# Adding the edge terms of a gathered message on VectorE instead of TensorE

## The reference

```python
def _L1_gnn_ref(H, Xe, id_Xe, M_W, M_b, U_W, U_b):
    features = H[id_Xe[0]]
    M_in = jnp.concatenate([features, Xe], axis=1)
    Y = jax.nn.relu(M_in @ M_W.T + M_b)
    Z = jax.ops.segment_sum(Y, id_Xe[1], num_segments=H.shape[0])
    U_in = jnp.concatenate([H, Z], axis=1)
    H_next = jax.nn.relu(U_in @ U_W.T + U_b)
    return H_next
```

## Time and profile before

| | |
|---|---|
| time, median of three runs | 26277.79 us (26254.98 to 26295.2) |
| the profiled execution: time | 26277.79 us |
| its span | 26276.0 us |
| PE busy | 9716.5 us (37%) |
| DVE busy | 9902.9 us (38%) |
| ACT busy | 1687.5 us (6%) |
| POOL busy | 15440.7 us (59%) |
| second gather layer, first gather to last block add | 4960 us |

### The profile page before, as it was taken

How to read it: one execution, slowest core, us unless ns; L and a number is a source line. 1 busy time by engine, 2 the same in 40 slices (tenths; PEclk the granted TensorE clock), 3 DMA queues, 4 the chain that set the end, 5 groups by cost and what they waited for, 6 DMA issues and landing times. The chain is left out here.

```text
span 26276.0 us, 210259 instructions
## 1 busy us (share of the span) xinstructions
PE 9716.5 (37%) x49375; PEld 7209.6 (27%) x49376; DVE 9902.9 (38%) x24717; ACT 1687.5 (6%) x4834; POOL 15440.7 (59%) x16460
## 2 busy tenths in 40 slices
PE   2555555423333333344343453333333111111146
PEld 1323232223333332222222223333333111111145
DVE  6666666533333333222222232222223222222257
ACT  4000000000000000000000010000000111111101
POOL 2666666666666664666666526666665666666610
PEclk7555555555555555666666665555555555555578
DMA  3222222222222222122121222222222222222255
GB/s 96 80 79 79 79 78 71 61 55 54 54 54 54 53 56 39 50 52 53 50 52 48 49 97 53 54 54 56 54 56 46 72 72 72 71 71 71 71 167 186
DMA packets 1005339, 1785.55 MB, mean 68 GB/s; under 512 B 352516, under 2 KB 461345, under 8 KB 1004756
## 3 DMA queue, kind: packets, MB, share of 16 engines
q1 hardware_dynamic: 484516, 1127.73, 13.6%
q0 software_dynamic: 513696, 654.80, 11.1%
q10 hardware_dynamic: 7056, 2.21, 0.0%
HBM read 1279.39 MB, written 510.79 MB: 68 GB/s over the span
## 5 line engine op out<-in xcount | busy, mean ns | idle before, releaser
L935 POOL DMA_INDIRECT arena<-table,arena x6464 | 6097.8, 943 | 3198.4 <-issue 1935.7
L1033 PE MATMUL psum<-arena 128*128 128x64 f32 x19392 | 4036.8, 369 | 8949.8 <-issue 7855.4
L1033 PEld LDWEIGHTS psum<-arena 128*128 128x128 f32 x19392 | 3960.5, 293 | 9289.3 <-issue 8978.6
L986 DVE TENSOR_TENSOR arena<-arena,psum 128x64 f32 x9696 | 2152.4, 222 | 9615.8 <-remote 4340.2
L700 POOL DMA_INDIRECT rec<-arena x3125 | 2991.6, 957 | 2284.4 <-issue 1847.9
L1150 POOL DMA_INDIRECT rec<-arena x3232 | 3178.9, 984 | 1770.2 <-issue 953.8
L935 POOL DMA_INDIRECT arena<-ptable,arena x3232 | 3048.9, 943 | 1871.2 <-issue 968.9
L477 PE MATMUL psum<-arena 128*128 128x196 bf16 (+1 forms) x4375 | 1378.6, 429 | 2174.4 <-DVE arena L608 1307.3
L1228 PE MATMUL psum<-arena 128*128 x3232 | 589.3, 362 | 3845.1 <-DVE arena L1177 2516.1
L1177 DVE CAST arena<-psum 128x1536 bf16<-128x1536 f32 x404 | 710.2, 1758 | 3407.8 <-remote 3352.6
L1228 PEld LDWEIGHTS psum<-arena 128*128 128x128 bf16 x3232 | 352.6, 109 | 4038.9 <-issue 3951.1
(11 more groups left out here) (198 smaller groups left out, 10158.6 us busy)
## 6 DMA issues: line engine op xcount, KB each, us to landing
arena<-rec SPq DMA_DIRECT2D x303, 1408.0 KB
arena<-rec SPq DMA_DIRECT2D x440, 488.0 KB
arena<-in_edge SPq DMA_DIRECT2D x625, 232.0 KB
arena<-rec SPq DMA_DIRECT2D x404, 352.0 KB
arena<-table,arena POOLq DMA_INDIRECT x6464
rec<-arena POOLq DMA_INDIRECT x6357
table<-arena SPq DMA_DIRECT2D x196, 512.0 KB
arena<-ptable,arena POOLq DMA_INDIRECT x3232
```

Of the source, the lines that this page charges most:

```text
L935: nc.gpsimd.indirect_dma_start(rows[q][:, j * D:(j + 1) * D], None, tab, bass.IndirectOffsetOnAxis(ap=idx[:, j, field:field + 1], axis=0)) ...
L986: v.tensor_tensor(block_sum, block_sum, ps[q % SB][:, j * D:(j + 1) * D], ALU.add).then_inc(s_add[j], 1)
L1033: last = nc.tensor.matmul(ps[q % SB][:, j * D:(j + 1) * D], hot[q % SB][:, j * P:(j + 1) * P], rows[q][:, j * D:(j + 1) * D], start=True, ...
```

## The change

The sum of gathered row and record term is made by the DVE, in place in `rows[q]`, as one 128x512 add (`add_terms`). It stands in the DVE's order of a group behind the one-hots of the group two on and ahead of the block adds of the group before. ACT takes the relu in place, from SBUF to SBUF. PE keeps only the products, in the same order in all layers. SP's wait for the one-hots of a block's last group is replaced by the wait for its sum in the second layer, which the DVE now gives. The banks `ps_q` and the parameter `ident` go.

```diff
-    ps_q = [psum[:, 512 * (SB + 1 + k):512 * (SB + 2 + k)] for k in range(2)]
...
-                    wait_earlier(sp, s_hot[q], i)
-                    if relu_q:
-                        wait_earlier(sp, s_sum[q], i)
+                    wait_earlier(sp, s_sum[q] if relu_q else s_hot[q], i)
...
+            def add_terms(i, q):
+                r = recs[q].rearrange("p (j w) -> p j w", w=RW)
+                mine = rows[q].rearrange("p (j f) -> p j f", f=D)
+                dve.wait_ge(s_g[q], i * (16 * G) + 16 * G)
+                v.tensor_tensor(mine, mine, r[:, :, R_Q:RW], ALU.add).then_inc(s_sum[q], 1)
+
             def step(i, groups=RG):
                 for q in range(groups):
                     if groups == RG or q + AHEAD < groups:
                         one_hots(i + (q + AHEAD) // RG, (q + AHEAD) % RG)
+                    if relu_q:
+                        add_terms(i, q)
                     if q:
                         add_group(i, q - 1)
...
                         act.wait_ge(s_sum[q], i + 1)
-                        nc.scalar.activation(rows[q], ps_q[q % 2], ACT.Relu).then_inc(s_msg, 1)
+                        nc.scalar.activation(rows[q], rows[q], ACT.Relu).then_inc(s_msg, 1)
...
-            def add_terms(i, q):
-                n = i * RG + q
-                pe.wait_ge(s_g[q], i * (16 * G) + 16 * G)
-                wait_earlier(pe, s_msg, n - 1)
-                nc.tensor.matmul(ps_q[q % 2], ident, rows[q], start=True, stop=False)
-                nc.tensor.matmul(ps_q[q % 2].rearrange("p (j f) -> p j f", f=D), ident,
-                                 recs[q].rearrange("p (j w) -> p j w", w=RW)[:, :, R_Q:RW], start=False, stop=True).then_inc(s_sum[q], 1)
...
             def step(i, groups=RG):
                 for q in range(groups):
+                    n = i * RG + q
+                    pe.wait_ge(s_hot[q], i + 1)
                     if relu_q:
-                        add_terms(i, q)
-                        if q:
-                            products(i, q - 1)
-                        elif not isinstance(i, int) or i:
-                            products(i - 1, RG - 1)
+                        pe.wait_ge(s_msg, n + 1)
                     else:
-                        products(i, q)
+                        pe.wait_ge(s_g[q], i * (16 * G) + 16 * G)
+
+                    wait_earlier(pe, s_add[G - 1], n - (SB - 1))
+                    for j in range(G):
+                        last = nc.tensor.matmul(ps[q % SB][:, j * D:(j + 1) * D], hot[q % SB][:, j * P:(j + 1) * P],
+                                                rows[q][:, j * D:(j + 1) * D], start=True, stop=True)
+                    last.then_inc(s_mm, 1)
```

More of the change, by code:

```diff
@@ L156, in build @@
         hparts, acc2 = shared.bitcast(BF16), shared[:, 0:NB * MW]
-        gather_layer(nc, sem, "g0", Buffers(arena, b.at), psum, iotaf, ident, blkd, acc, rec, table, R_GIDX, True, False)
+        gather_layer(nc, sem, "g0", Buffers(arena, b.at), psum, iotaf, blkd, acc, rec, table, R_GIDX, True, False)
         sem.end_stage()
@@ L160, in build @@
         sem.end_stage()
-        gather_layer(nc, sem, "g1", Buffers(arena, b.at), psum, iotaf, ident, blkd, acc, rec, ptable, R_SRC, False, True)
+        gather_layer(nc, sem, "g1", Buffers(arena, b.at), psum, iotaf, blkd, acc, rec, ptable, R_SRC, False, True)
         sem.end_stage()
@@ L166, in build @@
         sem.end_stage()
-        gather_layer(nc, sem, "g2", Buffers(arena, b.at), psum, iotaf, ident, blkd, acc, rec, table, R_GIDX, False, False)
+        gather_layer(nc, sem, "g2", Buffers(arena, b.at), psum, iotaf, blkd, acc, rec, table, R_GIDX, False, False)
         sem.end_stage()
@@ L883, in _, with gather_layer @@
                 step(last_pair, False)
-def gather_layer(nc, sem, name, b, psum, iotaf, ident, blkd, acc, rec, table, field, weighted, relu_q):
+def gather_layer(nc, sem, name, b, psum, iotaf, blkd, acc, rec, table, field, weighted, relu_q):
     loads = [b.take(LG * G * RW) for _ in range(RG // LG)]
@@ L1014, in _ @@
         def _(pe):
-            def add_terms(i, q):
-                n = i * RG + q
-                pe.wait_ge(s_g[q], i * (16 * G) + 16 * G)
-                wait_earlier(pe, s_msg, n - 1)
-                nc.tensor.matmul(ps_q[q % 2], ident, rows[q], start=True, stop=False)
-                nc.tensor.matmul(ps_q[q % 2].rearrange("p (j f) -> p j f", f=D), ident,
-                                 recs[q].rearrange("p (j w) -> p j w", w=RW)[:, :, R_Q:RW], start=False, stop=True).then_inc(s_sum[q], 1)
[L1023 to L1035, removed]
             def step(i, groups=RG):
                 for q in range(groups):
+                    n = i * RG + q
+                    pe.wait_ge(s_hot[q], i + 1)
                     if relu_q:
-                        add_terms(i, q)
-                        if q:
-                            products(i, q - 1)
-                        elif not isinstance(i, int) or i:
-                            products(i - 1, RG - 1)
-                    else:
-                        products(i, q)
+                        pe.wait_ge(s_msg, n + 1)
+                    else:
+                        pe.wait_ge(s_g[q], i * (16 * G) + 16 * G)
[4 more added lines that the diff above has]
+                    last.then_inc(s_mm, 1)
             peeled(pe, TURNS, step)
             step(TURNS, REST)
-            if relu_q:
-                products(TURNS, REST - 1)
 def update_stage(nc, sem, a, b, psum, ident, x, acc, h):
```

## The result

The kernel after took 26610.3 us (median of 4 runs, 26588.8 to 26618.9) against 26286.5 us before on the same chip (4 runs): ratio 1.0124, 95% interval 1.0106 to 1.0141, or 324 us more. The forecast was 26580 us, in a range of 26180 to 26870. The profiled execution had a span of 26630.0 us, 354 us more than the one before (26276.0).

A forecast was written before the change was run, and what follows sets the result against it. POOL's waits were taken to set the second gather layer's time; the later load and tail gave 252 to 290 us, taken as 300 with what both counts omit: 26278 + 300 = 26580 us, range 26180 to 26870.

The forecast's parts named there:

- What sets the layer's time: Second gather layer: what POOL waits for sets its time, 902 us of waits against 611 in the third layer.
- The wait that is moved: SP's load release in the second layer: 4.4 and 7.0 us later in two places, mean 5.7 us.
- The two counts: Later load in the second layer: 43 waits x 5.7 = 245 us, or 5.6 x 50.5 patterns = 283 us.
- The pattern of eight groups: POOL's stops per two loads: 9.85 us, then 13.6, together 23.5 us in eight groups against 17.9 before.
- The split of the waits: POOL in the second layer: waits for loads grow from 471.6 to some 750 us, for products stay at 430.
- The DVE's step in a burst: DVE in the second layer after a restart: 5.16 us a group becomes 5.9 with the new add.
- three new adds stand in the DVE's way: First place examined: 3 x 0.73 us of adds since the restart help let the load go 4.4 us later.
- the second count: Count by the pattern of eight groups: 23.5 us against 17.9, 5.6 x 50.5 = 283 us more.
- The add's price: New DVE add of 128x512 fp32 in the second layer: 688 ns, 0.73 us with the wait ahead of it.
- a gain of the change as written: Faster rival: second layer falls to the third's time, POOL's waits 902 to 611 us, 25994 us; chance 0.17.
- The tail: After POOL's last gather the DVE has some ten groups in hand, each 0.73 us longer: 7 us.
- The port: Rival: adds with two SBUF inputs block POOL's gathers, 279 us, 26557 us, or 26860 with the forecast on top; chance 0.08.

The follow-up runs named there:

- its removal in two different ways: Kernel after with the DVE's add made two groups ahead, ratio 0.9882; kernel after with second-layer loads of two groups instead of four, ratio 0.9898.
- the first: Kernel before, PE keeping the adds, SP's second-layer load also waiting for a small DVE memset where the change puts its add: 26755.1 us, ratio 1.0119.
- the fourth experiment: Kernel after with the add's second input taken from PSUM instead of SBUF, the record's term left out: 26669.0 us, ratio 1.0092.
- the terms ahead: Kernel after, but the DVE adds the terms of group q+2 right behind that group's one-hots: 26105.1 us, ratio 0.9882.
- the run made for it: Terms added two groups ahead, plus PE's eight records per group put back unused: 22713.2 us, ratio 1.0042; run again, 22696.2 us, 1.0046.
- 20 places: 20 places for groups instead of 12 in all gather layers, with the terms two groups ahead: 22702.2 us, ratio 1.0036.
- the repeat on the faster chip: Kernel after itself, unchanged, measured again where the kernel before took 22593.7 us: 22681.9 us, ratio 1.0039.
- the first four experiments: Later release alone, terms two groups ahead, loads of two groups, add's input from PSUM; run on one chip where before took 26428.5 us.
- the run with the marker in the third layer: Kernel before with loads released later, by a small DVE memset behind the one-hots two groups on, in the third gather layer alone: 22620.9 us, ratio 1.0000.

## Why the prediction was right

The time lies 30 us from the forecast, and the wait that the forecast rests on is the one that costs it. The sizes of its parts came out less well, and some of the errors cancel.

**What sets the layer's time.** Right: POOL's waits rose by 335 us and the layer by 382.

**The wait that is moved.** Right, and shown by itself: the later release alone gives 1.0119, its removal in two different ways gives 0.9882 and 0.9898. The two counts had 245 and 283 us for it; POOL's waits rose by 335. As forecast, the load is issued right behind the add of the block's last group.

**The pattern of eight groups.** Forecast 9.85 + 13.6 = 23.5 us of waits in eight groups; measured 1237 / 50.5 = 24.5. The mean hides two kinds: the pairs are 23.5 us, as drawn, though from other parts than drawn (see the DVE's step below), and more than half of the places are single stops of 26.4, which the pattern did not have. Where the add's second input comes from PSUM the pattern came in full (9.9 + 13.6).

**The split of the waits.** Off: 750 us for loads and 430 for products were forecast, 1053 and 184 measured. In the 27 single stops POOL stands at the load for the time that it would have stood at the product: the one wait hides behind the other. Only the sum was right.

**The DVE's step in a burst.** Wrong: 5.16 us should have become 5.9. Its one-hots start at 11592.50, 11597.63 and 11603.13, 5.1 and 5.5 us apart (5.25 over the five steps from 11592.50 to 11618.73). Before, the DVE stood idle some 1.2 us ahead of its block adds, put down to "issue" (it reads their eight places from memory); the idle time ahead of them is 0.62 us now. The add of 0.68 us lies in that gap. So in the step "three new adds stand in the DVE's way" the 0.73 us were mis-sized, they are near 0.1 a group. With 5.25 us in place of 5.9 the second count would have given 1.3 us less at each of 50.5 places, 66 us. That the sum came out all the same is luck in part. In 18 of the 22 pairs, and in all 48 of the run with the input from PSUM, the DVE stands before the load is let go, 2.5 us on average in that run, until a product of PE is made; the count had no such wait. And the 27 single stops are some 3 us longer than a pair.

**The add's price.** 0.688 us from the line through two rows; 684 ns measured. Hidden, as said. **ACT:** 630 ns, hidden.

**PE and the port, two terms put at nothing.** The sum had nothing for the work that PE loses and nothing for the port. On the slower chip PE's part was worth some 86 us with the late load (the first against the fourth experiment), and the port cost about as much, as far as ratios from two chips can be compared: 1.0124 against 1.0092. That they cancel is luck. With the terms ahead the second layer falls to the third's length, 1.2% under before. How much of this is the earlier load, how much PE's eight records and how much the post that PE no longer gives stays open: the run made for it fell on chips without stops. What did not come is a gain of the change as written; the late load hid it.

**The tail.** Seven us were added for the groups in hand after POOL's last gather. Measured, 53.0 us before and 53.8 after: under 1.

**The port.** The mechanism was given 0.08 and called not borne out, on one overlapping pair of rows. It is real, and the sign named for it came (gathers over 943 ns, here 956): the Trainium skill ("SBUF — State Buffer", section "Who interferes with whom") has it that such an instruction contends with a GpSimd instruction that reads SBUF, and the runs agree: 944 ns with the input from PSUM, 971 from SBUF. The size is not the rule's whole length: 88 us on the faster chip where the forecast's upper figure was 279, as only some gathers start while an add runs. Those lose nearly what is left of it, 0.41 us where they start 0.1 to 0.2 us into it. Nor does the later one always wait for what is left of the other: in the repeat on the faster chip an add that starts while a gather runs takes 700 ns on average, 723 at most, where 692 is the least. In the kernel after on the chip of the prediction the gathers themselves were 32 us longer for it (3090.1 busy against 3057.7 in the third layer), so it was no main term there. The error of the step was in the pair it looked at: that transfer started 0.21 us into an add of 0.29, so only 0.08 us of the add was left, and no more than that could be lost; gathers of the kernel after that start with so little left take 946 ns. The same stage of the trace before had the answer, at the DVE instruction behind that one, also with two SBUF inputs (L1173):

```profile
...
23804.35 0.30 DVE L1173 TENSOR_TENSOR arena<-arena 128x136 bf16<-128x136 f32 x1
23804.41 1.09 POOL L1150 DMA_INDIRECT rec<-arena  x1 [0.30 <-issue]
...
```

The 29 transfers of that stage that start 0.06 to 0.15 us into such an instruction take 1.01 to 1.09 us; the other transfers shown there and in the earlier trace rows take 0.98.

## What to carry to other kernels

When an instruction that frees a buffer moves to another engine, count where it stands in that engine's order, not only how long it takes: here a 0.7 us add cost 324 us because two groups of other work stood ahead of it, and the same add two groups earlier, with the loads then let go earlier than ever, gained 323. A ring of buffers is only as deep as its latest release. And read a loss on the machine that has it: where POOL never waited, the same edit cost a quarter as much and for another reason, and the terms-ahead version that wins 1.2% on one chip loses 0.4 to 0.5% on the others (measured there with 20 places and with PE's extra records, not alone).

## What the runs showed of the hardware

**The same program took 26255 to 26441 us in the runs of the result and of the first four experiments, and 22591 to 22634 on the two chips of the others.** In the slower runs PE goes through long stretches in which each of its records starts some 1.4 us behind the last. In the kernel before, on the first chip, PE's matmuls of the adds with their weight loads:

```profile
...
11560.19 1.01 PE L1019 MATMUL psum<-arena 128*128 128x512 f32 x1 [2.52 <-issue]
...
11561.59 0.29 PEld L1019 LDWEIGHTS psum<-arena 128*128 128x128 f32 x1 [2.51 <-issue]
...
11563.00 1.01 PE L1019 MATMUL psum<-arena 128*128 128x512 f32 x1 [1.79 <-issue]
...
11564.40 0.29 PEld L1020 LDWEIGHTS psum<-arena 128*128 128x128 f32 x1 [2.51 <-issue]
...
11566.49 1.01 PE L1020 MATMUL psum<-arena 128*128 128x512 f32 x1 [2.49 <-issue]
...
```

and in the run with the marker in the third layer, on a faster chip, at the same work (the add's second half, the products and the relu of the group):

```profile
...
10000.77 1.91 PE L1027 MATMUL psum<-arena 128*128 128x512 f32 x2
...
10002.47 2.08 PE L1040 MATMUL psum<-arena 128*128 128x64 f32 x16
...
10002.72 0.60 ACT L1016 ACTIVATE arena<-psum 128x512 f32<-128x512 f32 x1 [9.49 <-PE psum L1027]
...
```

From the first to the last of these records 6.3 us pass on the slower chip; on the faster one the two matmuls of a line took 1.91 us together, and the relu follows PE 0.04 us after their end. On the slower chip the relu often starts long after the sum that it waits for: in the kernel before, 154 of the 404 relus began more than 5 us after the end of the group's last L1020 matmul, up to 83 us; in the run on the faster chip all 404 began 0.04 us after it. And the DVE and POOL restart together, 9.85 us, 9.80 us and, in the kernel after, 9.42 us after POOL has stopped. What these stretches are (what PE's records wait for) was not settled; that they do not come from the program alone is shown by the faster chips.

**A gather and an add of two SBUF inputs on the DVE.** Gathers of the kernel after, grouped by how far into an add they start (means): 0.1 to 0.2 us 1354 ns, 0.2 to 0.3 us 1236, 0.3 to 0.4 us 1156, 0.4 to 0.5 us 1067, 0.5 to 0.6 us 953. Below 0.1 us it depends: in the repeat on the faster chip the 111 gathers that start less than 0.04 us into the add take 944 ns, those from 0.05 us on 1414 to 1455. A gather that runs already when the add starts takes 946, so it loses nothing, and the add takes 700 ns on average there. The adds that are held up more, 743 ns on average and up to 768 instead of 692, are those with a gather that starts in their first 0.05 us. With one input in PSUM no gather took over 971 ns.
